# A Mamba-2 mixer and a dequantised FFN in one kernel: the hand-written order of the mixer's steps is replaced

## The chip, the cores and the metric

One core of one Trainium2 chip runs the whole program. The metric is the device time of one execution in microseconds (us), as the median of three runs.

## What is computed

The input is 16 sequences of 256 tokens with 256 features, all in fp32. Each token goes through a Mamba-2 mixer, a residual sum, a layer norm, an FFN, a second residual sum and a second layer norm. The FFN's weights arrive as 4-bit codes with one scale for each block of 32.

```python
z, xBC, dt = split(u @ W_in)
xBC = silu(causal_conv4(xBC) + conv_b)
x, B, C = split(xBC)
dt = softplus(dt + dt_bias)
y = ssd(x * dt, -exp(A_log) * dt, B, C) + x * D
y = y * silu(z)
h = layernorm(u + (rmsnorm(y) * norm_scale) @ W_out)
out = layernorm(h + (gelu(h @ Wg.T) * (h @ Wu.T)) @ Wd.T)
```

Wg, Wu and Wd are the dequantised weights, with 2048 hidden units. The products keep fp32 accuracy: each factor is split into a high part and a rest (`_hi`, `_lo`), and three matmuls replace one (helper `mm3`, lines L540 to L542).

## The kernel before

**Groups.** The tokens are cut into nine groups: FIRST (number -1, one sequence, 2 tiles of 128 tokens), groups 0 to 6 (two sequences, 4 tiles each) and LAST (number 7, 2 tiles). Groups 1 to 6 are the steady ones; 1 to 5 are a hardware loop. While the mixer of group g runs, the FFN of group g-1 runs beside it. A group begins, in this text, where its predecessor's transposes "F1" (L660) stand: they turn the normed rows for the FFN. So the FFN of a 2-tile group runs beside the mixer of group 0.

**Units.** The FFN has 16 units. A unit is, on PE, the products into `gate_bank`, then those into `up_bank`, then the `down` products of the unit two before. ACT makes for it `in_hi` of the unit before (L789) and the GELU of this one (L803); DVE makes `in_lo` of the unit before (L1068) and the product gate times up (L1082). The gate products of unit n wait for the GELU of unit n-1, the up products for DVE's product of unit n-1, the down products for `in_lo`.

**Slots.** The mixer's steps stand by name in `SLOTS`, a list of 17 lists. `stages` turns it into one sequence: slot n, then unit n, slot n+1, unit n+1 and so on. Every engine walks through this one sequence and issues its own part of each step, so a step's place decides the order on all engines at once. Each engine works strictly in its order. The steps are:

- `x4`, `x5`, `x0` to `x3`: one input projection on PE (six matmuls of 512 columns), a bias and first tap on ACT (L738), three convolution taps (L937) and a SiLU (L868, tanh on ACT L722, both a projection or more later) on DVE. The last SiLU hangs on `z3`.
- `z0` to `z3`: one projection on PE, a tanh on ACT (L751), one product on DVE (L950).
- `CB0`, `CB1`: the products of B and C (L579, L581), masked on DVE (L956, L957), one copy on ACT (L757).
- `A`: the running sums (L596, L598), exponentials on ACT (L761, L762), copies on DVE (L962 to L965). SP then writes the sums to DRAM (`spread`, L451) and reads them back broadcast to all partitions as `low` (L460) and `dec` (L465).
- For tile i: `H` eight relus on ACT in place in `dec` (L770), after the landing of `dec`; `L` an addition on DVE (L971); `X` an exponential on ACT (L775); `XT` transposes on PE (L588) and a product on DVE (L976); `W` the product with CB on DVE (L982, L1042, L986); `Y` the products on PE (L607, for odd tiles also L617) and the sums on DVE (L998 to L1005); `g` squares and the split on ACT and DVE (L778, L783, L1009 to L1013); `S` the mean square (L624, L1024, POOL L1175); `op` the output projection and the residual on DVE (L1020).
- `ln1`, `ln2`: the layer norm's statistics and its application (L1050, L1054, POOL L1162 and L1164, L1062).

**Banks.** `USES` gives the order of the 32 products that go through four PSUM banks in turn: use n waits until use n-4 was read. `LINKS` hangs the 22 small steps of softplus (`dt`) between the convolution taps on DVE; the last one, `dA` (L921), releases `A`.

**Weights.** The 24 chunks of FFN weights are dequantised in the first two groups, on items of the same lists: `DECODE` and `VALUE` on DVE (L1106 to L1113, L1124), `UPPER` and `LOWER` on ACT (L810, L814), `TAKE_OFF` on PE (L689, L691). From chunk 13 on, PE's part of chunk c waits for ACT's `LOWER` of chunk c-1. `WOUT_AT` names the step behind which ACT scales and splits the output weights (L829, L832) in FIRST. Four constants set where among SP's scale loads the other transfers of these groups stand.

Of the kernel before, what the change touches and what calls it, by code (L numbers as in the profile page):

```python
# [57 lines left out]
VALUE = {FIRST: {"win": [0, 1], "x5": [2], "x0": [3], "A": [4], "x2": [5], "L0": [6], "XT0": [7], "X1": [8], "g0":
         [9, 10], "g1": [11], "S1": [12]}, 0: {0: [13], "x0": [14], "x1": [15], "CB0": [16], "A": [17,
         18], "L0": [19], "H1": [20], "L1": [21], "L2": [22], "S0": [23]}}  # L60
UPPER = {FIRST: {"win": [0], "x0": [1], "z0": [2, 3], "A": [4], "z3": [5], "W0": [6, 7], "W1": [8], "S0": [9],
         "op0": [10], "op1": [11, 12]}, 0: {"x5": [13], 1: [14], "z1": [15], "x2": [16], 4: [17, 18],
         "X0": [19], 7: [20], "g0": [21], "W2": [22], "g1": [23]}}
TAKE_OFF = {FIRST: {"x4": [0], "x1": [1], "z0": [2], "x3": [3], "z3": [4], "H1": [5], "W1": [6], "Y0": [7], "XT1":
         [8], "g1": [9, 10], "op1": [11], "ln1": [12]}, 0: {"x0": [13], "CB0": [14], "x2": [15], "x3":
         [16], 4: [17], "X0": [18], "Y0": [19], "W1": [20], 9: [21], "XT3": [22], 13: [23]}}
LOWER = {FIRST: {"z0": [0, 1], "x2": [2], "z2": [3], "L0": [4], "X0": [5], "Y1": [6, 7], "S1": [8, 9], "ln1": [10,
         11], "ln2": [12]}, 0: {"z0": [13], "CB1": [14], 3: [15], "x3": [16], "H0": [17], "Y0": [18],
         "H1": [19], "Y1": [20], "Y2": [21], "W3": [22], 14: [23]}}
# [1196 lines left out]
```

How the kernel before makes its waits and increments, by code:

```python
def wait(eng, signal, group, k):  # L125
    value = signal.at(group, k)
    if not isinstance(value, int) or value > 0:
        eng.wait_ge(signal.sem, value)
# [278 lines left out]
        @block.sync  # L408
# [1 line left out]
            def load_block(b):  # L410
                if b:
                    sp.wait_ge(decoded.sem, b)
                sp.dma_start(packed[:, :], ffn_w[:, b, :]).then_inc(packed_in.sem, 16)
# [1 line left out]
            def load_scales(c):  # L415
                if c >= 2:
                    sp.wait_ge(valued.sem, c - 1)
                sp.dma_start(scales[:, c % 2, :], ffn_s[:, c, :]).then_inc(scales_in[c % 2].sem, 16)
# [20 lines left out]
            def wait_for(*rises):  # L439
                values = [s.at(group, k) for s, group, k in rises]
                values = [v if isinstance(v, int) else sp.to_reg(v) for v in values]
                sp.wait_ge(wout_in.sem, 16)
                for (s, _, _), v in zip(rises, values):
                    sp.wait_ge(s.sem, v)
# [1 line left out]
            def spread_sums(g, which=range(NT)):  # L448
# [5 lines left out]
                    if i >= 2:
                        wait_for((exp_in, g, i - 1))
                    elif kind_of(g) == "first" and i:
                        sp.wait_ge(winz_ok.sem, JT)
                    sp.dma_start(low[:, i % 2, :, :], of_tile(1, i).partition_broadcast(P)).then_inc(lo_in[i % 2].sem, 16)
                    if i >= 2:
# [40 lines left out]
                if c == KEEP_FIRST:  # L502
                    sp.wait_ge(wt_lo.sem, BESIDE_FIRST)
                    keep_h(FIRST)
```

## Time and profile before

| | |
|---|---|
| median of three runs | 926.2 us (924.76 to 927.67) |
| the profiled execution's own time | 930.15 us |
| its span, first to last instruction | 928.4 us |
| PE busy | 858.1 us (92%) |
| PE weight loads | 742.8 us (80%) |
| DVE busy | 698.9 us (75%) |
| ACT busy | 554.3 us (60%) |
| POOL busy | 71.4 us (8%) |
| mean granted clock of PE | 0.978 |

Times are counted from the span's first instruction. A duration of PE includes a modelled tail that overlaps the next matmul, so the sum of its durations is more than its busy time, and the distance from one start to the next says how fast it works. "Idle before" is the engine's idle time ahead of a row, and behind it stands what ended it. The clock is the granted one, 1.00 being 2.4 GHz and 0.50 being 1.2 GHz.

### The profile page before, as it was taken

Reading aid. Unit: us, or ns where it says so; the run is one execution under the profiler, and the core shown is the slowest. Engines: PE = TensorE matmul, PEld = TensorE weight load, DVE = VectorE, ACT = ScalarE, POOL = GpSimd, SP = SyncE. Lnnn points to the kernel's source line nnn. Section 1 sums busy time; section 2 is a strip of 40 time slices with the busy share of each in tenths; the row PEclk is TensorE's granted clock in tenths of the full one; section 3 lists DMA queues with packets and bytes.
Section 4 is the critical chain, followed back from the end, with each engine's and each line's share of the span. In section 5 each row is a group of like instructions: output and inputs, shape, how many; then the busy total and the mean of one; then the engine's idle time right before and its main releaser. Section 6 shows DMA issues by size and latency. Waiting matters only on the chain.

```text
span 928.4 us, 16398 instructions
## 1 busy us (share of the span) xinstructions
PE 858.1 (92%) x5512; PEld 742.8 (80%) x5512; DVE 698.9 (75%) x1588; ACT 554.3 (60%) x1014; POOL 71.4 (8%) x105
## 2 busy tenths in 40 slices
PE   4669798899999999999999999999999999999997
PEld 3448677787898888887888789888888788888886
DVE  6776878787879688886878787877879687857453
ACT  4844687458735776548735775559636774566232
POOL 2110000200020000200020000200020000100000
PEclk9897989899999999999999999999999999999999
DMA  4421440015101420023001420133001410130010
GB/s 144 132 76 39 128 124 24 12 58 161 35 24 68 121 85 23 25 75 139 34 23 68 126 79 23 45 90 128 11 23 69 150 57 12 58 104 1 1 35 12
DMA packets 37578, 61.32 MB, mean 66 GB/s; under 512 B 3264, under 2 KB 25888, under 8 KB 37536
## 3 DMA queue, kind: packets, MB, share of 16 engines
q1 hardware_dynamic: 37104, 60.76, 20.5%
q8 instruction: 23, 0.38, 0.2%
q14 instruction: 19, 0.16, 0.1%
q10 hardware_dynamic: 432, 0.03, 0.0%
HBM read 51.94 MB, written 4.64 MB: 61 GB/s over the span
## 4 chain that ended last, share of the span: by engine, by line
PE 65%; DVE 10%; DMA 9%; issue 7%; ACT 5%; POOL 3%; SPq 1%; DVEq 0%; POOLq 0%; ACTq 0%
DMA dec<-spread 7%; PE gate_bank L540 5%; PE up_bank L540 5%; PE up_bank L542 5%; PE up_bank L541 5%; PE gate_bank L542 5%; PE gate_bank L541 5%; PE mixer L540 5%; PE down L540 4%; PE down L541 4%; PE down L542 4%; PE mixer L541 4%; PE mixer L542 4%; PE mixer L607 3%; ACT dec L770 2%
## 5 line engine op out<-in xcount | busy, mean ns | idle before, releaser
L540 PE MATMUL down<-wd_hi,in_hi 128*128 128x256 f32 x512 | 144.1, 282 | 0.7 <-DVE in_lo L1068 0.7
L541 PE MATMUL down<-wd_lo,in_hi 128*128 128x256 f32 x512 | 142.9, 279 | 0.0
L542 PE MATMUL down<-wd_hi,in_lo 128*128 128x256 f32 x512 | 142.6, 278 | 0.0
L937 DVE SCALAR_TENSOR_TENSOR xbc<-mixer,chan,xbc 128x510 f32<-128x510 f32 (+1 forms) x162 | 111.1, 686 | 25.2 <-ACT xbc L738 24.3
L540 PE MATMUL gate_bank<-hT_hi,wg_hi 128*128 128x512 f32 (+1 forms) x288 | 113.2, 393 | 11.4 <-ACT act_sb L803 11.4
L789 ACT ACTIVATE in_hi<-act_sb 128x512 fp32r<-128x512 f32 (+1 forms) x144 | 83.0, 576 | 64.1 <-PE down L542 53.0
L1082 DVE SCALAR_TENSOR_TENSOR act_sb<-up_bank,act_sb 128x512 f32<-128x512 f32 (+1 forms) x144 | 90.6, 629 | 39.9 <-PE up_bank L542 20.0
L1068 DVE TENSOR_TENSOR in_lo<-act_sb,in_hi 128x512 fp32r<-128x512 f32 (+1 forms) x144 | 90.2, 627 | 40.2 <-ACT in_hi L789 39.7
L540 PE MATMUL up_bank<-hT_hi,wu_hi 128*128 128x512 f32 (+1 forms) x288 | 107.0, 371 | 5.6 <-DVE act_sb L1082 5.6
L803 ACT ACTIVATE act_sb<-gate_bank 128x512 f32<-128x512 f32 (+1 forms) x144 | 79.0, 549 | 50.4 <-PE gate_bank L542 49.8
L542 PE MATMUL up_bank<-hT_hi,wu_lo 128*128 128x512 f32 (+1 forms) x288 | 107.0, 371 | 0.0
L542 PE MATMUL gate_bank<-hT_hi,wg_lo 128*128 128x512 f32 (+1 forms) x288 | 106.8, 371 | 0.0
L541 PE MATMUL gate_bank<-hT_lo,wg_hi 128*128 128x512 f32 (+1 forms) x288 | 106.5, 370 | 0.0
L541 PE MATMUL up_bank<-hT_lo,wu_hi 128*128 128x512 f32 (+1 forms) x288 | 106.4, 370 | 0.0
L540 PEld LDWEIGHTS down<-wd_hi,in_hi 128*128 128x128 f32 x512 | 96.9, 189 | 5.1 <-DVE in_lo L1068 1.1
L541 PEld LDWEIGHTS down<-wd_lo,in_hi 128*128 128x128 f32 x512 | 96.9, 189 | 4.3
L542 PEld LDWEIGHTS down<-wd_hi,in_lo 128*128 128x128 f32 x512 | 96.8, 189 | 0.0
L738 ACT ACTIVATE xbc<-mixer,chan 128x512 f32<-128x512 f32 (+1 forms) x54 | 39.5, 731 | 88.8 <-PE mixer L542 88.7
L770 ACT ACTIVATE dec<-dec,sum_hi 128x128 f32<-128x128 f32 x256 | 78.4, 393 | 13.1 <-DMA dec<-spread 13.1
L540 PE MATMUL mixer<-uT_hi,win_hi 128*128 128x512 f32 (+1 forms) x180 | 72.4, 402 | 13.0 <-DVE wdt L1142 9.5
L540 PEld LDWEIGHTS gate_bank<-hT_hi,wg_hi 128*128 128x128 f32 x288 | 54.7, 190 | 25.5 <-ACT act_sb L803 11.4
L1175 POOL TENSOR_TENSOR rms<-rms_v,minus_half 128x1 f32<-128x1 f32 x32 | 18.8, 588 | 710.2 <-DVE rms_v L1024 710.2
(183 smaller groups left out, 1868.5 us busy)
## 6 DMA issues: line engine op xcount, KB each, us to landing
low<-spread SPq DMA_DIRECT2D x32, 512.0 KB, 3.8
dec<-spread SPq DMA_DIRECT2D x32, 512.0 KB, 6.1
state_decay<-spread SPq DMA_DIRECT2D x32, 128.0 KB, 7.4
xbc<-in_u_t_dram SPq DMA_DIRECT2D x7, 512.0 KB, 3.7
h_sb<-in_u_dram SPq DMA_DIRECT2D x7, 512.0 KB, 3.8
h_res<-h_sb SPq DMA_DIRECT2D x7, 512.0 KB, 2.9
out_dram<-h_res SPq DMA_DIRECT2D x7, 512.0 KB, 2.9
scales<-in_ffn_s_dram SPq DMA_DIRECT2D x24, 128.0 KB, 2.2
```

The lines of the kernel that those rows point to most:

```text
L540: nc.tensor.matmul(dst, lh, rh, start=first, stop=False, skip_group_check=True)
L541: nc.tensor.matmul(dst, lh, rl, start=False, stop=False, skip_group_check=True)
L542: return nc.tensor.matmul(dst, ll, rh, start=False, stop=last, skip_group_check=True)
L607: mm = nc.tensor.matmul(bank(g, use)[a * HP:(a + 1) * HP, j * P:(j + 1) * P], xdt[:, h * HP:(h + 1) * HP], dec[:, i % 2, h, :], start=True ...
L738: nc.scalar.activation(xbc[:, i, 0:width(g)], bank(g, f"x{i}")[:, 0:width(g)], ACT.Identity, bias=chan[:, 24 + i:25 + i], scale=chan[:, 18 ...
L770: ins = nc.scalar.activation(at, at, ACT.Relu, bias=sum_hi[:, c:c + 1], scale=-1.0)
L789: nc.scalar.activation(in_hi[:, n % 2, 0:width(f)], act_sb[:, n % 2, 0:width(f)], ACT.Copy)\
L803: nc.scalar.activation(act_sb[:, n % 2, 0:width(f)], GB[:, 0:width(f)], ACT.Gelu_apprx_tanh, scale=CODE_SCALE).then_inc(gelu_ok.sem, 1)
L937: ins = stt(acc[:, :, d:], src[:, :, 0:SEQ - d], chan[:, c:c + 1], acc[:, :, d:], ALU.mult, ALU.add)
L1068: tt(in_lo[at], act_sb[at], f32(in_hi[at]), ALU.subtract)\
L1082: stt(inter, UB[:, 0:width(f)], CODE_SCALE, inter, ALU.mult, ALU.mult)\
L1175: tt(rms[:, i:i + 1], rms_v[:, i:i + 1], half[:, 0:1], ALU.pow).then_inc(rms_ok.sem, 1)
```

## The change

It changes tables only, no instruction's code. In the steady groups (`"full"`) z0 and z1 stand one slot sooner, CB0 one later and CB1 three later, x2 one sooner, z3 one later. H0 stays in slot 5, now behind CB1 and z3, with L0 in the same slot. H1 and H2 stand at the front of their slots, and XT1, L1, g0, L2, X2, H3, op0, g1, S1, op1 and S2 stand one slot sooner. In group 0 (`"second"`) H0 and L0 stand a slot sooner, and S3, op3 and ln1 are in slot 14, with slot 15 empty. FIRST gets a new order too: A and CB0 sooner, z3 ahead of H0, XT0 ahead of L0. The five tables of weight chunks and `LINKS` are written anew for these orders; every chunk is still made once, and chunk block 5 is decoded at the end of FIRST instead of in group 0. LAST is untouched.

```diff
-    "full": ["dt", "x4", "x5", "x0", "z0", "x1", "CB0", "CB1", "z1", "x2", "z2", "A", "x3", "z3", "XT0", "Y0", "XT1",
...
+    "full": ["dt", "x4", "x5", "z0", "x0", "z1", "x1", "x2", "z2", "CB0", "A", "x3", "CB1", "z3", "XT0", "Y0",
...
-    "full": [["x5"], ["x0", "z0"], ["x1", "CB0", "CB1", "z1"], ["x2", "z2"], ["A", "x3", "z3"], ["H0"],
-             ["L0", "XT0", "X0", "W0"], ["Y0", "H1"], ["L1", "XT1", "X1", "W1"], ["Y1", "g0", "H2"],
...
+    "full": [["x5", "z0"], ["x0", "z1"], ["x1", "x2"], ["z2", "CB0"], ["A", "x3"], ["CB1", "z3", "H0", "L0"],
+             ["XT0", "X0", "W0"], ["H1", "Y0", "XT1", "L1"], ["X1", "g0", "W1"], ["H2", "L2", "Y1", "XT2", "X2"],
...
-    "second": [[], ["x5", "x0", "z0"], ["x1", "CB0", "CB1", "z1"], ["x2", "z2"], ["A", "x3"], ["z3"], ["H0",
-               "L0", "XT0", "X0", "W0"], ["Y0", "H1", "L1", "XT1"], ["X1", "W1"], ["Y1", "g0", "H2", "L2",
...
+    "second": [[], ["x5", "z0", "x0"], ["z1", "x1", "x2"], ["z2", "CB0"], ["A", "x3", "CB1", "z3"], ["H0",
+               "L0"], ["XT0", "X0", "W0"], ["H1", "Y0", "XT1", "L1"], ["X1", "g0", "W1", "H2"], ["L2", "Y1",
...
+               ["Y3", "S2"], ["op2", "g3"], ["S3", "op3", "ln1"], [], ["ln2"]],
...
-DECODE = {FIRST: {"win": [1], "x2": [2], "XT1": [3], "S0": [4]}, 0: {"x0": [5], 3: [6], "z3": [7]}}
...
+DECODE = {FIRST: {"win": [1], "A": [2], "L0": [3], "g0": [4], "ln2": [5]}, 0: {"z2": [6], "z3": [7]}}
...
-WOUT_AT = "x3"
...
+WOUT_AT = "X1"
...
-SPREAD_FIRST, NEXT_UT, KEEP_FIRST, SPREAD_NEXT = 6, 14, 15, 20
+SPREAD_FIRST, NEXT_UT, KEEP_FIRST, SPREAD_NEXT = 6, 13, 17, 20
```

The order of ACT's instructions in a steady group, from A's exponentials (L761) on, before:

```order
L761 ACTIVATE xtail<-mixer3 32x128
L762 ACTIVATE low_exp<-mixer3 128x32
L738 ACTIVATE xbc<-mixer0,chan 128x512
L722 ACTIVATE y<-xbc 128x512 x2
L751 ACTIVATE zs<-mixer1 128x512
L789 ACTIVATE in_hi<-act_sb 128x512
L803 ACT_TABLE_LOAD
L803 ACTIVATE act_sb<-gate_bank 128x512
L770 ACTIVATE dec<-dec,sum_hi 128x128 x8
```

and with the change (its lines are one higher, since a line was added to a table):

```order
L762 ACTIVATE xtail<-mixer2 32x128
L763 ACTIVATE low_exp<-mixer2 128x32
L739 ACTIVATE xbc<-mixer3,chan 128x512
L723 ACTIVATE y<-xbc 128x512
L790 ACTIVATE in_hi<-act_sb 128x512
L804 ACT_TABLE_LOAD
L804 ACTIVATE act_sb<-gate_bank 128x512
L758 ACTIVATE cb<-mixer0 128x128
L723 ACTIVATE y<-xbc 128x512
L752 ACTIVATE zs<-mixer1 128x512
L771 ACTIVATE dec<-dec,sum_hi 128x128 x8
```

The GELU of unit 4 stood behind the last tanh and z3's; now these two and CB1's copy stand between it and the relus of tile 0.

DVE's instructions in a steady group between x1's last tap and the product of unit 2 (L1082), before:

```order
L868 SCALAR_TENSOR_TENSOR xbc<-y,xbc 128x512
L956 TENSOR_TENSOR cb<-mixer2,tri 128x128
L957 TENSOR_TENSOR cb<-mixer2,tri 128x128
L956 TENSOR_TENSOR cb<-mixer3,tri 128x128
L957 TENSOR_TENSOR cb<-mixer3,tri 128x128
L950 SCALAR_TENSOR_TENSOR zs<-zs,mixer0 128x512
L908 SCALAR_TENSOR_TENSOR dtp<-dtp,dts 128x32
L1068 TENSOR_TENSOR in_lo<-act_sb,in_hi 128x512
L1082 SCALAR_TENSOR_TENSOR act_sb<-up_bank,act_sb 128x512
```

and with the change:

```order
L869 SCALAR_TENSOR_TENSOR xbc<-y,xbc 128x512
L938 SCALAR_TENSOR_TENSOR xbc<-mixer3,chan,xbc 128x2x255
L907 SCALAR_TENSOR_TENSOR dtp<-dtp,dtq 128x32
L938 SCALAR_TENSOR_TENSOR xbc<-mixer3,chan,xbc 128x2x254
L938 SCALAR_TENSOR_TENSOR xbc<-mixer3,chan,xbc 128x2x253
L909 SCALAR_TENSOR_TENSOR dtp<-dtp,dts 128x32
L869 SCALAR_TENSOR_TENSOR xbc<-y,xbc 128x512
L1069 TENSOR_TENSOR in_lo<-act_sb,in_hi 128x512
L1083 SCALAR_TENSOR_TENSOR act_sb<-up_bank,act_sb 128x512
```

CB0, CB1 and the z product left this place, and the taps and the SiLU of x2 came in.

ACT's instructions in group 0 around the relus of tile 0, before:

```order
L751 ACTIVATE zs<-mixer1 128x512
L789 ACTIVATE in_hi<-act_sb 128x256
L803 ACTIVATE act_sb<-gate_bank 128x256
L770 ACTIVATE dec<-dec,sum_hi 128x128 x8
L814 ACTIVATE wd_lo<-down1 128x512
```

and with the change:

```order
L811 ACTIVATE wd_hi<-act_sb 128x512
L811 ACTIVATE wg_hi<-h_res 128x2x256
L815 ACTIVATE wd_lo<-down1 128x512
L771 ACTIVATE dec<-dec,sum_hi 128x128 x8
L790 ACTIVATE in_hi<-act_sb 128x256
L804 ACTIVATE act_sb<-gate_bank 128x256
```

The copy `wd_lo` of chunk 17, for which PE's part of chunk 18 waits, stood behind the relus and stands ahead of them now; one unit's GELU went the other way.

## Rows read from the trace of the kernel before

**Rows 1.** Busy time by stretch: window, busy and (count) of PE, PEld, DVE, ACT, POOL, clock, DMA.
```profile
0.00:67.70 67.70, 40.00 (x199) 27.60 (x199) 51.05 (x134) 38.64 (x84) 11.04 (x26) 0.92 0.39 117
67.70:172.19 104.49, 88.76 (x575) 74.91 (x575) 79.77 (x189) 67.89 (x135) 9.05 (x10) 0.91 0.24 72
...
379.40:483.00 103.60, 101.10 (x650) 87.84 (x649) 81.74 (x180) 64.82 (x114) 7.85 (x11) 1.00 0.18 66
...
791.70:928.40 136.70, 122.77 (x857) 112.07 (x856) 80.08 (x200) 59.74 (x119) 7.51 (x12) 0.97 0.11 36
```

**Rows 2.** Waits of the whole run: who waited for whom, total us, times, longest.
```profile
PE gate_bank L540 <- ACT act_sb L803: 11.4, 9, 1.7
...
PE mixer L607 <- DVE dec L986: 6.3, 9, 1.1
```

**Rows 3.** Timeline of PE in group 3: start, duration, what, [idle before, released by].
```profile
410.76 0.38 PE L596 MATMUL mixer<-tri,dA 128*96 128x128 f32 x2
...
411.12 0.48 PE L540 MATMUL mixer<-uT_hi,win_hi 128*128 128x512 f32 x1
...
414.01 0.40 PE L540 MATMUL gate_bank<-hT_hi,wg_hi 128*128 128x512 f32 x1
...
419.64 0.50 PE L540 MATMUL gate_bank<-hT_hi,wg_hi 128*128 128x512 f32 x1 [1.33 <-ACT act_sb L803]
...
429.64 1.09 PE L607 MATMUL mixer<-dec,xdt 128*64 128x128 f32 x16 [0.89 <-DVE dec L986]
```

**Rows 4.** Timeline of ACT over the same stretch of group 3.
```profile
411.35 0.27 ACT L761 ACTIVATE xtail<-mixer 32x128 f32<-32x128 f32 x1 [1.25 <-PE mixer L598]
...
416.04 0.63 ACT L722 ACTIVATE y<-xbc 128x512 f32<-128x512 f32 x1 [1.93 <-DVE xbc L937]
...
417.70 1.28 ACT L803 ACT_TABLE_LOAD   x1
418.99 0.60 ACT L803 ACTIVATE act_sb<-gate_bank 128x512 f32<-128x512 f32 x1
420.81 2.46 ACT L770 ACTIVATE dec<-dec,sum_hi 128x128 f32<-128x128 f32 x8 [1.22 <-DMA dec<-spread]
```

**Rows 5.** Timeline of DVE in group 3, 398 to 431 us.
```profile
401.57 0.28 DVE L956 TENSOR_TENSOR cb<-mixer,tri 128x128 f32<-128x128 f32 x1
...
403.66 0.69 DVE L1082 SCALAR_TENSOR_TENSOR act_sb<-up_bank,act_sb 128x512 f32<-128x512 f32 x1
406.23 0.75 DVE L937 SCALAR_TENSOR_TENSOR xbc<-mixer,chan,xbc 128x510 f32<-128x510 f32 x1 [1.88 <-ACT xbc L738]
...
428.27 1.22 DVE L986 TENSOR_TENSOR dec<-dec,cb 128x1024 f32<-128x1024 f32 x1
```

**Rows 6.** Timeline of ACT in group 0, 98 to 124 us.
```profile
113.27 2.45 ACT L770 ACTIVATE dec<-dec,sum_hi 128x128 f32<-128x128 f32 x8 [2.33 <-DMA dec<-spread]
```

**Rows 7.** Timeline of PE in group 0, 98 to 178 us.
```profile
101.32 0.43 PE L596 MATMUL mixer<-tri,dA 128*96 128x128 f32 x2 [1.16 <-DVE dA L921]
...
116.34 2.04 PE L689 MATMUL down<-h_res,ident 128*128 128x512 f32 x2 [3.97 <-ACT wd_lo L814]
...
172.19 1.13 PE L660 MATMUL gate_bank<-ident,h_sb 128*128 128x128 f32 x4 [3.56 <-DVE h_sb L1062]
```

**Rows 8.** Busy time by stretch, after the stall of group 0.
```profile
115.60:122.40 6.80, 6.06 (x21) 4.92 (x21) 5.19 (x8) 6.74 (x13) 0.00 (x0) 0.50 0.19 43
```

**Rows 9.** Timelines at the norm's last step: DVE and POOL in group 0, DVE in group 3.
```profile
168.87 3.27 DVE L1062 TENSOR_SCALAR h_sb<-h_sb,mv,lnr 128x256 f32<-128x256 f32 x4 [0.93 <-POOL lnr L1164]
...
168.99 2.68 POOL L1171 TENSOR_TENSOR uT_lo<-xbc,uT_hi 128x512 fp32r<-128x512 f32 x2 [0.23 <-ACT uT_hi L731]
...
481.33 1.39 DVE L1062 TENSOR_SCALAR h_sb<-h_sb,mv,lnr 128x256 f32<-128x256 f32 x4 [0.36 <-POOL lnr L1164]
```

**Rows 10.** Timelines of ACT, then DVE, in the first group, 30 to 45 us.
```profile
35.06 2.45 ACT L770 ACTIVATE dec<-dec,sum_hi 128x128 f32<-128x128 f32 x8 [0.83 <-DMA dec<-spread]
...
37.84 0.43 DVE L868 SCALAR_TENSOR_TENSOR xbc<-y,xbc 128x256 f32<-128x256 f32 x1 [2.27 <-ACT y L722]
```

More of the change, by code:

```diff
@@ L26 @@
 USES = {
[3 rows of a table removed]
+    "full": ["dt", "x4", "x5", "z0", "x0", "z1", "x1", "x2", "z2", "CB0", "A", "x3", "CB1", "z3", "XT0", "Y0",
+             "XT1", "Y1", "Yoff0", "XT2", "S0", "op0", "Y2", "S1", "XT3", "op1", "Y3", "Yoff1", "S2", "op2",
+             "S3", "op3"],
+    "first": ["dt", "x4", "x5", "x0", "z0", "A", "CB0", "x1", "z1", "x2", "x3", "z2", "z3", "XT0", "Y0", "XT1",
               "Y1", "Yoff0", "S0", "op0", "S1", "op1"],
@@ L56 @@
 BESIDE_FIRST = 13
-DECODE = {FIRST: {"win": [1], "x2": [2], "XT1": [3], "S0": [4]}, 0: {"x0": [5], 3: [6], "z3": [7]}}
[L58 to L69, printed above, removed]
@@ L71 @@
-LINKS = {4: {("x4", 1): [3], ("x4", 2): [4], ("x4", 3): [5], ("x5", 1): [6], ("x5", 2): [7], ("x5", 3): [8],
[2 rows of a table removed]
+DECODE = {FIRST: {"win": [1], "A": [2], "L0": [3], "g0": [4], "ln2": [5]}, 0: {"z2": [6], "z3": [7]}}
+VALUE = {FIRST: {"win": [0, 1], "x5": [2], "x0": [3], "x1": [4], "x3": [5], "X0": [6], "W0": [7], "W1": [8],
+         "XT1": [9], "g0": [10], "g1": [11], "S1": [12]}, 0: {0: [13], "z0": [14, 15], "x1": [16], "A":
+         [17], "CB1": [18], 4: [19], "X0": [20], "H1": [21], "W1": [22], "g1": [23]}}
@@ new lines @@
+UPPER = {FIRST: {"x4": [0], "x0": [1], "A": [2], "CB0": [3], "x3": [4], "L0": [5], "X0": [6], "Y0": [7], "Y1":
+         [8], "g0": [9], "op0": [10], "S1": [11], "op1": [12]}, 0: {"x5": [13], "z1": [14], "z2": [15],
+         "CB1": [16], 4: [17, 18], "X0": [19, 20], 8: [21], "Y2": [22], "S1": [23]}}
+TAKE_OFF = {FIRST: {"x4": [0], "x0": [1], "z1": [2], "x3": [3], "z3": [4], "H1": [5], "W1": [6], "XT1": [7], "Y1":
+         [8], "g1": [9, 10], "ln1": [11, 12]}, 0: {"x0": [13], "x2": [14], "CB0": [15], "z3": [16], 4:
+         [17], 5: [18], "H1": [19], 7: [20], "X2": [21], "Y2": [22], "g2": [23]}}
@@ new lines @@
+LOWER = {FIRST: {"z0": [0], "z1": [1], "z2": [2], "XT0": [3], "H1": [4], "X0": [5], "g0": [6], "op0": [7], "op1":
+         [8, 9, 10], "ln2": [11, 12]}, 0: {"z1": [13], "z2": [14], "CB1": [15], "z3": [16], 4: [17],
+         "XT0": [18], "XT1": [19], "Y1": [20], "op0": [21], "XT3": [22], 11: [23]}}
+LINKS = {4: {("x4", 1): [3], ("x4", 2): [4, 5], ("x5", 1): [6], ("x0", 1): [7], ("x0", 2): [8, 9, 10],
+             ("x0", 3): [11], ("x1", 1): [12], ("x1", 2): [13, 14], ("x2", 1): [15], ("x2", 3): [16], ("z2", 0): [17, 18,
+             19, 20, 21]},
```

15 rows, old and new, of tables (LINKS, SLOTS, USES) are left out of this document.

## The prediction

> **What bounds the kernel now.** I read the busy time by stretch first [rows 1]. The profile's page puts PE at 92% busy, and a steady group shows it plainly: in group 3 PE is busy 101.10 of 103.60 us at a clock of 1.00, DVE 81.74 and ACT 64.82. So in the six steady groups PE sets the time, and all that an order can give back there is PE's idle time, 2.5 us a group. The two groups ahead are another matter: FIRST has PE busy 40.00 of 67.70 us, and DVE with 51.05 is the fullest engine; group 0 has 88.76 of 104.49 at a clock of 0.91. Together they leave over 40 us idle. LAST and the end (136.70 us) are not touched.
>
> The waits name the idle time [rows 2]: PE's gate products wait for a GELU (11.4 us, 9 times) and its Y products for DVE's `dec` (6.3 us, 9 times). PE's timeline shows one of each in group 3 [rows 3]: 1.33 us before the gate products of unit 5, 0.89 us before Y0. Nothing else there is worth a term.
>
> ACT's timeline says why the first comes [rows 4]. After A (411.35) ACT stands before the last tanh (416.04) until DVE has done x3's taps, an idle time of 1.93 us; then z3, `in_hi`, a table load, and only at 418.99 the GELU of unit 4. After it ACT waits 1.22 us more for the landing of `dec` and does tile 0's relus until 423.27.
>
> **The steady groups.** PE's products are the same, so only waits change. I walk through the new order.
>
> *Slot 2.* x1 and x2 now follow each other. DVE loses the two CBs here (four products, each up to 0.28, about 0.8 us) and gains x2's three taps at 0.75 and its SiLU (0.69, the length of the other 512-wide products), about 3.0 us [rows 5]. Its product for unit 2 starts at 403.66 and ends at 404.35; 2.2 us on is 406.6. PE wants it for unit 3's up products. These and the `down` products behind them stand right before A (410.76), and each third of a unit takes 1.4 us: unit 4 begins at 414.01, and 1.33 us of idle time end at 419.64, so it ends at 418.3 [rows 3]. So they begin at about 408.0 now, and at 407.3 without CB1 ahead. Room: 0.7 us. DVE's idle 1.88 us before x2 [rows 5] is what paid for it. Price nothing; the bound is 1.5 us a group, if DVE is late by twice that room.
>
> *Slots 4 and 5.* Unit 4's GELU no longer stands behind the last tanh and z3. The gate products of unit 5 find it done: 1.33 us gone, with the little that PE takes to start again. But the landing of `dec` is now the chain. From A's exponentials (411.35) to the landing (420.81) it is 9.46 us [rows 4], all of it transfers and their waits, and and the new order makes A sooner only by CB1's products on PE. No row prices these alone: between nothing and a projection's 1.45 us (two take 411.12 to 414.01, [rows 3]); with half the columns I take half of it, 0.7. H0 then starts at about 420.1, ends at 422.6, and unit 5's GELU, behind it on ACT as before, ends at 423.6. PE would be there 0.9 us before. So at unit 6's gate products **0.7 us** are won, not 1.33: a new wait of 0.9 us takes the place of the old.
>
> *Y0.* It waited for W0 (428.27, 1.22 us, [rows 5]), which came late behind `in_lo` and the product of unit 5 (0.69 each), both ahead of L0. L0 now stands ahead of them. W0 ends sooner by the 0.7 of the landing and some 0.6 of these two, at 428.2; the rest of Y0's wait is 0.3. PE stands **1.3 us** ahead there.
>
> *Behind it* H2 and H3 wait for transfers that SP may issue only after Y0 and Y1, so they move with them. X2 loses its stand behind Y1 on DVE, and F1 keeps its distance from op3 (same slots). I keep 1.2 of the 1.3: six groups, **-7.2 us**. Bounds: -2.5 each, all of PE's idle time, and +1.5 each from slot 2.
>
> **Group 0.** Two stalls carry it [rows 7]. At 116.34 PE had stood 3.97 us, since chunk 18 waits for ACT's `wd_lo` of chunk 17, which stood behind H0; H0 itself waited 2.33 us for `dec` and took 2.45 [rows 6]. Now that copy is ahead of H0. In its place unit 6's gate products wait for the GELU behind H0. A comes sooner, too: DVE has one chunk block less to decode before it and both CBs, and A had waited 1.16 us for DVE [rows 7]. I take **-3.5** for this: the nearest row is 3.97, less the new wait, plus A's gain. Bounds 0 (the wait only moves) and -7 (with the clock). After the stall the clock stood at 0.50, that is 1.2 GHz, for the whole stretch of 6.80 us, in which PE was busy 6.06 [rows 8]; at 2.4 GHz that work would take 3.0 less. I leave this out of the sum, since a wait of some two us stays in this place.
>
> The Trainium skill, "TensorE: Matmul & The Clock Gate", section "HAM oscillation", says that a wait long enough puts the engine back to half its clock, and that each such wait is paid again in slow matmuls. By that rule a stall that gets shorter wins the slow stretch too: -6.5 for this term where I have -3.5, and 908 for the whole.
>
> The other is at the end: F1 waits 3.56 us for the layer norm [rows 7]. Its last step took 3.27 us for four instructions, against 1.39 in group 3; POOL's `uT_lo` for the next group ran beside it (168.99, 2.68 us) [rows 9]. Now ln1 stands in slot 14 and a unit without mixer work follows, so the norm is done when PE comes and ahead of `uT_lo`. **-3.0**, bounds 0 and -3.6.
>
> **FIRST.** DVE is the chain. It stood 2.27 us before the last SiLU, since ACT did H0's relus (35.06, 2.45) ahead of the tanh [rows 10]. z3 is ahead of H0 now, and ACT's split of the output weights has moved behind X1. Against it, block 5 is decoded here, after ln2, about 1.5 us partly in idle time, and L0 still waits for relus that themselves start later. **-1.5**, bounds -3 and +1.5.
>
> **Sum.** -7.2 - 3.5 - 3.0 - 1.5 = -15.2. The profiled execution took 930.15 us of its own time, so it would take 915.0; it lies 3.95 above the median, and against the median of 926.2 the sum gives **911.0 us**.
>
> **Rivals.**
>
> *The wait only changes its name.* The `dec` transfers land later than 9.46 us after A, since other transfers now meet them, or H3's do. Then the steady groups give nothing and the first two their 8.0: 918.2. For it: three of the five steps on this path are transfers, whose time I can't see inside. Against: their neighbours in the queue don't change. 0.15.
>
> *Slower: DVE becomes the engine that PE waits for in slot 2.* Two sets of taps and two SiLUs run in a row there, with 0.7 us of room. If DVE enters slot 2 more than 0.7 us later than I have it (z0 and z1 are sooner as well), every further tenth is paid by PE at unit 3, and A and with it `dec` slip as well. At 2 us late, 1.3 is paid at unit 3 and the landing takes back the rest: +1.3 for each steady group, +7.8, and in group 0, where DVE is fuller, the 8.0 are lost: 934. It decides from a PE wait before unit 3's up products above 1.2 us. 0.13.
>
> *Nothing in sum:* the steady groups lose what the first two win, 926. 0.07.
>
> *More than I say, by the clock.* The stall in group 0 gets short enough that PE stays at 2.4 GHz, which wins the 3.0 us of [rows 8], and the steady groups win half a us more each, for which the landing of `dec` would have to come 0.5 us sooner: 905. For it: 0.50 stands in the trace right behind the longest wait. Against: another wait remains there. 0.05. The page of the skill named above would have the first half of this happen.
>
> **How the numbers follow.** The forecast itself, from 905 to 917, has 0.60. I call 0.3% (2.8 us) what a measurement of this kernel can tell. Faster is 0.60 + 0.15 + 0.05 = 0.80, less some of the second's weak end: 0.79. Same 0.08, slower 0.13. The range from 903 to 923 takes in the forecast, its bounds up to both clock and a weak DVE, and the first rival; it leaves out the slower one and some of the third.
>
> **What would show it.** In a steady group of the changed kernel: no PE wait before unit 5's gate products, one of about 0.9 before unit 6's, Y0's wait under 0.5, a group 1.2 us shorter than the 103.60 of group 3. In group 0: no PE wait for `wd_lo`, F1's wait under 1 us, its last norm step near 1.4. FIRST ends near 66. I am wrong if a wait for DVE stands before unit 3's up products, if H0's wait for `dec` on ACT grows past 2 us, or if PE waits before F1 in the steady groups.

## The result, and the profile after

The changed kernel takes **910.94 us** (median of 5 runs, 910.7 to 912.51) where the kernel before, timed beside it, takes 927.67 (5 runs, 924.76 to 929.48): ratio 0.9822, 95% interval 0.9804 to 0.9841, so 14.7 to 18.2 us less. A second set gave 912.8 against 927.67 us, ratio 0.9832 (0.9809 to 0.9855). The forecast was 911.0 us, range 903 to 923. The profiled execution took 912.18 us with a span of 910.4, against 930.15 and 928.4.

Busy time by stretch of the changed kernel: FIRST, group 0, group 3, LAST with the end (columns as in [rows 1]; every line number is one higher than before).

```profile
0.00:66.92 66.92, 43.80 (x200) 30.94 (x200) 51.77 (x135) 38.62 (x84) 11.23 (x26) 0.87 0.40 118
66.92:166.75 99.83, 88.62 (x576) 74.54 (x576) 80.45 (x189) 67.52 (x135) 7.30 (x9) 0.91 0.25 76
369.70:471.00 101.30, 100.91 (x649) 87.61 (x649) 82.21 (x180) 65.08 (x114) 8.51 (x11) 1.00 0.21 68
774.70:910.40 135.70, 121.35 (x858) 110.78 (x856) 79.94 (x200) 59.71 (x119) 7.58 (x12) 0.98 0.10 36
```

PE's idle time in group 3 went from 2.50 us (103.60 less 101.10, [rows 1]) to 0.39; the busy times of that group's PE, DVE and ACT are within 0.5 us of what they were. In FIRST PE is busy 3.8 us longer, at a clock of 0.87 where it had 0.92. The 18.0 us between the two spans lie so, by the starts of F1:

| stretch | before | after | difference |
|---|---|---|---|
| FIRST | 67.70 | 66.92 | -0.8 |
| group 0 | 104.49 | 99.83 | -4.7 |
| group 1 | 103.87 | 101.12 | -2.7 |
| groups 2 to 6 | 515.60 | 506.87 | -8.7 |
| LAST and end | 136.74 | 135.70 | -1.0 |

Waits of PE in the whole run (total us, times, longest), the two that [rows 2] shows of before:

```profile
PE gate_bank L541 <- ACT act_sb L804: 4.9, 6, 1.8
PE mixer L608 <- DVE dec L987: 4.7, 4, 2.0
```

The wait for `dec` is gone from the steady groups. Of the six waits for a GELU three still stand there, all before unit 6's gate products: 0.17 us in group 1, 0.59 in group 2 and 0.21 in group 6. PE's timeline of group 3, to be read against [rows 3]: unit 3's up products, then the gate products of units 4, 5 and 6, then Y0.

```profile
397.37 0.50 PE L541 MATMUL up_bank<-hT_hi,wu_hi 128*128 128x512 f32 x1
...
402.09 0.40 PE L541 MATMUL gate_bank<-hT_hi,wg_hi 128*128 128x512 f32 x1
...
408.28 0.40 PE L541 MATMUL gate_bank<-hT_hi,wg_hi 128*128 128x512 f32 x1
...
413.12 0.51 PE L541 MATMUL gate_bank<-hT_hi,wg_hi 128*128 128x512 f32 x1
...
417.72 1.09 PE L608 MATMUL mixer<-dec,xdt 128*64 128x128 f32 x16
```

None has a wait that the view prints; single instructions show 0.09 us at 413.12 and 0.07 at 417.72, where before there were 1.33 ahead of unit 5 and 0.89 ahead of Y0. ACT, against [rows 4]:

```profile
400.83 0.27 ACT L762 ACTIVATE xtail<-mixer 32x128 f32<-32x128 f32 x1 [1.07 <-PE mixer L599]
...
405.42 0.60 ACT L804 ACTIVATE act_sb<-gate_bank 128x512 f32<-128x512 f32 x1
...
409.61 2.46 ACT L771 ACTIVATE dec<-dec,sum_hi 128x128 f32<-128x128 f32 x8 [0.53 <-DMA dec<-spread]
...
412.50 0.57 ACT L804 ACTIVATE act_sb<-gate_bank 128x512 f32<-128x512 f32 x1
```

Unit 4's GELU stands at 405.42, 2.9 us ahead of the gate products that want its bank. From A's exponentials (400.83) to the landing (409.61) it is 8.78 us, 9.46 before. Unit 5's GELU, behind H0, ends at 413.07, and PE is there. DVE, against [rows 5]: the product of unit 2, L0, W0.

```profile
396.63 0.68 DVE L1083 SCALAR_TENSOR_TENSOR act_sb<-up_bank,act_sb 128x512 f32<-128x512 f32 x1
...
412.10 1.23 DVE L972 TENSOR_TENSOR dec<-dec,low 128x1024 f32<-128x1024 f32 x1 [2.30 <-ACT dec L771]
...
416.36 1.22 DVE L987 TENSOR_TENSOR dec<-dec,cb 128x1024 f32<-128x1024 f32 x1
```

The product of unit 2 ends at 397.31 and PE starts unit 3's up products at 397.37. That is the 0.7 us of room of slot 2, used up.

In group 0, PE's waits, against [rows 7]:

```profile
96.39 1.10 PE L690 MATMUL down<-act_sb,ident 128*128 128x512 f32 x2 [1.13 <-ACT wd_lo L815]
...
115.47 0.36 PE L541 MATMUL gate_bank<-hT_hi,wg_hi 128*128 128x256 f32 x1 [1.77 <-ACT act_sb L804]
...
120.47 1.09 PE L608 MATMUL mixer<-dec,xdt 128*64 128x128 f32 x16 [0.90 <-DVE dec L987]
...
130.17 1.09 PE L608 MATMUL mixer<-dec,xdt 128*64 128x128 f32 x16 [2.01 <-DVE dec L987]
...
134.72 2.05 PE L690 MATMUL down<-act_sb,ident 128*128 128x512 f32 x2 [0.94 <-ACT wd_lo L815]
...
166.75 0.74 PE L661 MATMUL gate_bank<-ident,h_sb 128*128 128x128 f32 x4 [0.47 <-DVE h_sb L1063]
```

Chunk 18's wait of 3.97 us is gone, the GELU wait of 1.77 has come in its place, and two waits for `dec` follow. PE also waits four times for ACT's copies of other chunks, 3.4 us in sum: the two rows with `wd_lo`, and 0.60 and 0.76 us at 104.52 and 109.57. F1 waits 0.47 where it waited 3.56. The norm's last step (DVE) and POOL's `uT_lo` there, against [rows 9]:

```profile
165.32 1.37 DVE L1063 TENSOR_SCALAR h_sb<-h_sb,mv,lnr 128x256 f32<-128x256 f32 x4
166.68 2.72 POOL L1172 TENSOR_TENSOR uT_lo<-xbc,uT_hi 128x512 fp32r<-128x512 f32 x2 [2.02 <-ACT uT_hi L732]
```

The step takes 1.37 us and is over before `uT_lo` begins; it took 3.27 beside it.

### The profile page after: what moved, and what is told of

Same layout as the page of the kernel before. It is cut to its first block, busy times and chain, and to the rows that moved or that the text cites. A ratio compares the mean times of both kernels' runs of the same rounds, so it can differ in the third digit from the quotient of the medians.

```text
span 910.4 us, 16399 instructions
## 1 busy us (share of the span) xinstructions
PE 858.1 (94%) x5512; PEld 741.5 (81%) x5512; DVE 703.0 (77%) x1588; ACT 555.9 (61%) x1014; POOL 76.8 (8%) x105
## 4 chain that ended last, share of the span: by engine, by line
PE 71%; DMA 7%; DVE 7%; issue 6%; ACT 5%; POOL 3%; SPq 1%; POOLq 0%; DVEq 0%; ACTq 0%
PE gate_bank L541 6%; PE up_bank L541 5%; PE gate_bank L543 5%; PE up_bank L543 5%; PE gate_bank L542 5%; PE up_bank L542 5%; DMA dec<-spread 5%; PE mixer L541 5%; PE down L541 5%; PE down L542 5%; PE down L543 5%; PE mixer L543 4%; PE mixer L542 4%; PE mixer L608 4%; ACT dec L771 2%
## 5 line engine op out<-in xcount | busy, mean ns | idle before, releaser
L541 PE MATMUL gate_bank<-hT_hi,wg_hi 128*128 128x512 f32 (+1 forms) x288 | 111.0, 386 | 5.1 <-ACT act_sb L804 4.9
L1083 DVE SCALAR_TENSOR_TENSOR act_sb<-up_bank,act_sb 128x512 f32<-128x512 f32 (+1 forms) x144 | 90.3, 627 | 26.7 <-PE up_bank L543 22.1
L541 PE MATMUL mixer<-uT_hi,win_hi 128*128 128x512 f32 (+1 forms) x180 | 72.4, 402 | 12.6 <-DVE wdt L1143 8.8
L1176 POOL TENSOR_TENSOR rms<-rms_v,minus_half 128x1 f32<-128x1 f32 x32 | 23.8, 745 | 675.6 <-DVE rms_v L1025 675.6
L541 PEld LDWEIGHTS up_bank<-hT_hi,wu_hi 128*128 128x128 f32 x288 | 54.4, 189 | 18.5 <-DVE act_sb L1083 9.4
```

The costliest lines, as they stand in the source:

```text
L541: nc.tensor.matmul(dst, lh, rh, start=first, stop=False, skip_group_check=True)
L1083: stt(inter, UB[:, 0:width(f)], CODE_SCALE, inter, ALU.mult, ALU.mult)\
L1176: tt(rms[:, i:i + 1], rms_v[:, i:i + 1], half[:, 0:1], ALU.pow).then_inc(rms_ok.sem, 1)
```

## The experiments

Twelve kernels, all timed in five rounds beside the kernel before. The sets' medians of before are 927.28 us (the first four), 926.56 (the next four) and 927.67 (the last four); ratios are to these.

| kernel | us | ratio to before, 95% interval |
|---|---|---|
| steady groups alone | 918.22 | 0.9904 (0.9889 to 0.9919) |
| first two groups alone | 920.24 | 0.9925 (0.9911 to 0.9938) |
| norm of group 0 late | 917.44 | 0.9895 (0.988 to 0.991) |
| L0 late | 916.86 | 0.9887 (0.9872 to 0.9902) |
| z3 beside A | 913.84 | 0.9861 (0.984 to 0.9882) |
| `wd_lo` of chunk 17 behind H0 | 913.23 | 0.9857 (0.9836 to 0.9878) |
| CB0 in slot 2 | 913.88 | 0.9866 (0.9848 to 0.9885) |
| LAST with A early | 907.27 | 0.9789 (0.977 to 0.9808) |
| the change again | 912.8 | 0.9832 (0.9809 to 0.9855) |
| H0 early in FIRST | 915.58 | 0.9864 (0.9844 to 0.9884) |
| block 5 decoded later | 914.76 | 0.9859 (0.984 to 0.9879) |
| LAST with slot 0 empty | 904.6 | 0.975 (0.9733 to 0.9767) |

### The two halves apart

The first kernel is the one before with the change's "full" lists (slots, banks, links) for groups 1 to 6; group 0 keeps its own. The second is the change with the old "full" lists for groups 1 to 6.

```diff
+def uses_of(g):
+    return "second" if isinstance(g, int) and g == 0 else kind_of(g)
...
-            return MB[USES[kind_of(g)].index(use) % 4]
+            return MB[USES[uses_of(g)].index(use) % 4]
```

> The new order in the six steady groups alone; FIRST, group 0, LAST as before. Theory (the parts are local and add up): groups 1 to 6 lose their idle time as in the changed kernel, 103.3 to 101.3 us in groups 2 to 6 and 1.0 in group 1, whose slow stretch behind F1's wait of 3.56 us stays: -9.7, so 917.5 against 927.2 us, ratio 0.9895. Rival 1 (only my forecast's 1.2 a group is the order's, the rest of what the changed kernel won came from a luckier landing of the dec transfers): 920, ratio 0.992. Rival 2 (the steady groups' gain hangs on the slow stretch being gone): groups 2 to 6 above 102.5 us each.

> The new lists for FIRST and group 0 (mixer steps and chunks) alone; groups 1 to 6 in their old order. Theory (the slow clock goes with the wait before F1): FIRST 66.9, group 0 99.8 and group 1 shorter by 1.7 through the clock, -7.2: 920.0 us, ratio 0.992. Rival (waits alone, the slow stretch comes anyway): -5.5, 921.7 and a granted clock of 0.5 somewhere from 165 to 175 us. Groups 2 to 6 stand at 103.3 with their 1.33 us before unit 5's gate products in both.

They gave -9.1 and -7.0 us, against -9.7 and -7.2 expected. The product of the ratios is 0.9830, the whole change 0.9822 and 0.9832: the halves add. Groups 1 and 3 of the steady groups alone:

```profile
171.20:276.90 105.70, 105.43 (x642) 91.91 (x643) 80.49 (x172) 64.72 (x113) 5.45 (x8) 0.94 0.19 64
...
378.90:480.30 101.40, 100.89 (x649) 87.63 (x648) 82.17 (x180) 65.06 (x114) 8.51 (x10) 1.00 0.21 68
```

Group 3 is as short as in the change, and groups 2 to 6 take 101.3 to 102.0 us, so neither rival of the first kernel holds. Group 1 is at 0.94: the wait of 3.56 us before F1 is there, and this time the clock stood at 0.50 from 169.9 to 183.6. With the first two alone that wait is 0.47 and no slow stretch stands anywhere near it, against the rival: group 1 took 102.92 us, 103.87 before, though PE's waits in it (2.02 us before, F1's left out) came to 2.89. So the clock gave back 1.8 (103.87 - 2.02 less 102.92 - 2.89).

### The norm of group 0

```diff
-["Y3", "S2"], ["op2", "g3"], ["S3", "op3", "ln1"], [], ["ln2"]]
+["Y3", "S2"], ["op2", "g3"], [], ["S3", "op3", "ln1"], ["ln2"]]
```

> The changed kernel with S3, op3 and ln1 of group 0 back in slot 15 and slot 14 left empty. Theory (the norm's place made F1's wait and the slow clock behind it): PE waits 3.0 to 3.6 us before F1, POOL's uT_lo stands beside the norm's last step, which takes about 3.3 us, and a stretch at 0.5 follows: +3.1 and +1.7, 915.7 us. Rival 1 (the stretch does not follow): +3.1, 914.0. Rival 2 (the wait was gone for another reason, DVE being ahead in the new order): under 1 us of wait, 911 to 912.

PE at F1, DVE's norm step, POOL's `uT_lo`, and the stretch at half clock, which begins in F1's wait and ends 4.6 us behind it:

```profile
169.29 1.12 PE L661 MATMUL gate_bank<-ident,h_sb 128*128 128x128 f32 x4 [3.56 <-DVE h_sb L1063]
```

```profile
165.96 3.27 DVE L1063 TENSOR_SCALAR h_sb<-h_sb,mv,lnr 128x256 f32<-128x256 f32 x4 [0.93 <-POOL lnr L1165]
```

```profile
166.09 2.68 POOL L1172 TENSOR_TENSOR uT_lo<-xbc,uT_hi 128x512 fp32r<-128x512 f32 x2 [0.23 <-ACT uT_hi L732]
```

```profile
167.10:173.90 6.80, 4.61 (x19) 4.32 (x20) 5.09 (x10) 1.20 (x2) 1.66 (x2) 0.50 0.00 0
```

All four came back with one edit: the wait of 3.56, the step of 3.27 and the overlap to the hundredth, and the half clock. Rivals 1 and 2 are out. In the fourteen traces of this study a slow stretch stands around F1 at the end of group 0 in the three where F1 waited 3.56 us (before, steady groups alone, this one) and in none of the eleven where it waited 0.5. The time rose by 6 us (ratio 0.9895 against 0.9822 and 0.9832) where 4.8 was expected; of the rest, 1.1 us of this trace lie in LAST, see below.

### The steady groups: what holds each wait away

```diff
-["CB1", "z3", "H0", "L0"], ["XT0", "X0", "W0"]
+["CB1", "z3", "H0"], ["L0", "XT0", "X0", "W0"]
```

> The changed kernel with L0 of tile 0 of the steady groups behind in_lo and the product of unit 5, as it was before. Theory (ACT's table load covers part of it: the exp could not start before 414.38 anyway, and L0 would end at about 415.05): W0 is 0.7 us later, PE waits 0.8 before Y0 in each of the six groups: +4.3, 915.2 us. Rival 1 (the two DVE instructions count in full with the gap before them, 1.7 us): +9.5, 920.4. Rival 2 (L0's place is worth nothing, PE takes the time elsewhere): 911 to 911.5.

```diff
-["A", "x3"], ["CB1", "z3", "H0", "L0"]
+["A", "x3", "CB1", "z3"], ["H0", "L0"]
```

> The changed kernel with CB1 and z3 of the steady groups back in slot 4, ahead of unit 4's products; H0 and L0 stay. Theory (the last tanh and z3 ahead of unit 4's GELU on ACT made the wait before unit 5's gate products, and dec lands as before, so PE has no slack at Y0): a PE wait of about 0.8 us before unit 5's gate products (1.33 less CB1's 0.57 of PE work that now stands ahead of it), the 0.1 waits before unit 6's and Y0 gone, +0.65 in each of six groups: +4, 915 us. Rival 1 (the place of z3 is worth its whole old wait): 1.33 each, +8, 919. Rival 2 (only where H0 and L0 stand counts; the wait before unit 5 is then taken out of those behind it): 911 to 912.

```diff
-["x1", "x2"], ["z2", "CB0"]
+["x1", "x2", "CB0"], ["z2"]
```

> The changed kernel with CB0 of the steady groups back in slot 2, behind x2: DVE gets two products of 0.28 us more there. In the trace of the changed kernel DVE ends the product of unit 2 at 397.31 and PE begins unit 3's up products at 397.37, so the room is nearly gone where my forecast had 0.7. Theory (no room): PE waits about 0.35 us before unit 3's up products in each of six groups, +2.1, 913.0 us. Rival (room of 0.7 as forecast, CB0 costs nothing): 911. A rival past both (A slips too and dec lands later, it is paid twice): 915.

With L0 late, PE's wait before Y0 is 0.87 to 0.89 us in each of the six groups (0.8 expected), and the sum of that name over the run is

```profile
PE mixer L608 <- DVE dec L987: 9.8, 10, 2.0
```

where the change has 4.7. Rivals 1 (1.7 us each) and 2 (nothing) are out; the time is 5 to 6 us above the change by the ratios, 4.3 expected. With z3 beside A, and with CB0 in slot 2, one line each from group 3:

```profile
408.20 0.50 PE L541 MATMUL gate_bank<-hT_hi,wg_hi 128*128 128x512 f32 x1 [0.64 <-ACT act_sb L804]
```

```profile
395.90 0.50 PE L558 MATMUL up_bank<-hT_hi,wu_hi 128*128 128x512 f32 x1 [0.31 <-DVE act_sb L1100]
```

0.64 us before unit 5's gate products (0.8 expected), the waits before Y0 gone; 0.31 before unit 3's up products (0.35 expected), where neither kernel had one. The second stands in groups 2 to 5 (0.29 to 0.31); in groups 1 and 6 the view prints none. The times are 913.84 and 913.88, +3 to +4 by the ratios, where +4 and +2 were expected; their intervals overlap with that of the change in the second set, so it is the two lines that decide. PE's waits in groups 1 to 6 rose by 2.2 and 1.8 us. Each of the three edits puts a price on the path at once. The new order stands where three chains reach PE at nearly the same time as it gets there: DVE's products in slot 2, the GELU behind the last tanh, and `dec`.

### Group 0: the copy and H0

```diff
-"z3": [16], 4: [17],
+"z3": [16], "H0": [17],
```

> The changed kernel with ACT's wd_lo copy of chunk 17 back behind H0 of group 0. My forecast (this edit is what took the wait of 3.97 us away): PE waits 2 to 4 us more for wd_lo at chunk 18 and the clock falls behind it: 914 to 918 us. Theory now (unit 5's GELU stands behind H0 on ACT as well and PE waits for it next, 1.77 us at 115.47, so the copy only adds its own length of 0.6 and the transposes that are pushed behind it): +1 to +1.5, 912 to 912.5. Rival (nothing at all, all of it taken out of the GELU wait): 911.

PE, then ACT, of this kernel:

```profile
114.41 2.04 PE L690 MATMUL down<-h_res,ident 128*128 128x512 f32 x2 [2.66 <-ACT wd_lo L815]
...
122.17 1.09 PE L608 MATMUL mixer<-dec,xdt 128*64 128x128 f32 x16 [1.22 <-DVE dec L987]
```

```profile
111.34 2.44 ACT L771 ACTIVATE dec<-dec,sum_hi 128x128 f32<-128x128 f32 x8 [1.73 <-DMA dec<-spread]
113.69 0.57 ACT L815 ACTIVATE wd_lo<-down 128x512 fp32r<-128x512 f32 x1
```

The wait for chunk 18 is back with 2.66 us, and another stands before Y0, 1.22. The group takes 101.70 us, and its part ahead of F1's wait 101.19, where the ten kernels with the change's lists for the first two groups take 98.11 in the mean (96.93 to 99.74, F1's wait left out): +3.1. The time rose by 2 to 3 us; 913.23 lies between the two expectations, 914 to 918 and 912 to 912.5. My forecast's mechanism stands, and the "theory now" of +1 to +1.5, by which the GELU wait would have taken most of it, is too low.

### FIRST, and block 5

```diff
-"z2", "z3", "H0", "XT0",        WOUT_AT = "X1"
+"z2", "H0", "z3", "XT0",        WOUT_AT = "x3"
```

> The changed kernel with H0 ahead of z3 in FIRST and ACT's split of the output weights back at x3, as both stood before. My forecast (DVE's 2.27 us of idle time before the last SiLU come back): FIRST 1.5 us longer, +1.5, 912.4 us. Rival (DVE is full in FIRST, 51 of 67 us in both kernels, and its other waits give back what this one costs): FIRST within 0.5 us from the point where DVE has a_neg, 911.

```diff
-DECODE = {FIRST: {..., "g0": [4], "ln2": [5]}, 0: {"z2": [6], ...
+DECODE = {FIRST: {..., "g0": [4]}, 0: {"x5": [5], "z2": [6], ...
```

> The changed kernel with the decoding of block 5 moved from behind ln2 of FIRST to behind x5 of group 0. Theory (behind ln2 it costs nothing, because PE then waits 1.9 us for POOL's uT_lo anyway; behind x5 its 1.5 us stand ahead of DVE's work for unit 0): +0.5 to +1.5, 911.5 to 912.5 us. Rival (as my forecast had it, it costs FIRST a part of its 1.5 us, and group 0 has room): -0.5 to -1, 910.

> The changed kernel itself once more, as the yardstick of the others in this set. 910.9 us as measured, within 1.5.

FIRST begins with loads whose arrival differs from run to run (DVE's first use of `a_neg` stands at 12.90 to 13.91 us), so I count from there to F1: 53.80 and 53.78 us in the two traces with the old list, 53.40 in the mean of the ten with the new one, which go from 52.58 to 54.22. With H0 and the split as before it is 56.63. PE's waits in it include the first two rows, and DVE's wait before the last SiLU is back (2.27 before, [rows 10]; none in the change):

```profile
35.17 0.50 PE L692 MATMUL gate_bank<-wu_hi,in_hi 128*128 128x512 f32 x1 [2.80 <-ACT wu_hi L811]
39.11 1.09 PE L589 MATMUL mixer<-ident,xbc 128*128 128x128 f32 x4 [3.44 <-DVE xbc L869]
...
38.54 0.42 DVE L869 SCALAR_TENSOR_TENSOR xbc<-y,xbc 128x256 f32<-128x256 f32 x1 [2.69 <-ACT y L723]
```

against 1.61 before the second in the change. So the places of H0 and of ACT's split together are worth 3.2 us of FIRST (the time: 915.58 against 912.8 in the same set); yet the whole list won 0.4, less than the spread of the ten. Something else in it costs some 2.8 us. Block 5 is not what cost it: with its decoding moved to group 0 FIRST is no shorter (54.38), group 0 is at 100.94 with a new wait of 1.47 us before an up product for DVE, and the time is 914.76, 2 us more (0.5 to 1.5 expected). Behind ln2 it is free. A part may be the clock: it stood at 0.50 for 10.2 and 13.7 us of FIRST with the old list, and for 13.7 to 20.5 with the new one. The two new ones at 13.7 take 52.6 and 52.7 us, the seven at 17.1 take 53.1 to 54.2, and the one at 20.5 takes 54.0. What makes the stretches longer, and which moves cost the rest, wasn't tried.

### LAST in the new order

LAST keeps its old list in the change. Two lists for it, on top of the change:

```diff
 "last":
-[["x5"], ["x0", "z0"], ["x1", "CB0", "z1"], ["x2", "z2"], ["A", "x3", "z3"], ["H0"], ["L0", "XT0", ...
+[["x5", "z0"], ["x0", "z1"], ["x1", "x2"], ["A", "z2", "CB0"], ["x3"], ["z3", "H0", "L0"], ["XT0", ...
```

> The changed kernel with LAST in the new order too, and A there a slot sooner than in the steady groups (LAST has half the mixer work of PE, so the transfers take more units than there). Theory (the same chain of A, transfers, relus, L0, W0 makes the waits of LAST: 0.55 and 1.63 us before gate products, 0.89 before Y0): they fall to under 0.6 in sum, -2.4, 908.5 us; the 2.23 us before unit 1's up products stay. Rival 1 (GELU and table loads on ACT make them, not the transfers): only Y0's goes, 910. Rival 2 (DVE is late in slot 2 with two sets of taps and PE waits 1 us or more before unit 3's up products): 911 to 912.

```diff
-[["x5", "z0"], ["x0", "z1"], ["x1", "x2"], ["A", "z2", "CB0"], ["x3"], ["z3", "H0", "L0"],
+[[], ["x5", "z0"], ["x0", "z1", "x1"], ["A", "x2", "z2"], ["CB0", "x3"], ["z3", "H0", "L0"],
```

> The changed kernel with LAST in the new order, its slot 0 empty, x5 to x1 pushed one slot on, and A in slot 3. Against the list with A early and x5 in slot 0 (907.3 us), which keeps a PE wait of 1.87 us before unit 1's up products, since DVE does x5's taps, z0 and the final norm ahead of unit 0's product. Theory (that queue on DVE makes the wait): the wait goes, 905.4 us. Rival 1 (the same work makes PE wait a unit later, before unit 2's up products): 907. Rival 2 (the final norm alone makes it): a wait over 1 us stays before unit 1's, 907.

Busy time of LAST in the first of these, then PE's only wait there, and LAST in the second:

```profile
773.40:860.90 87.50, 85.63 (x554) 76.29 (x553) 58.77 (x142) 46.54 (x85) 5.42 (x8) 0.98 0.13 43
```

```profile
786.36 0.52 PE L541 MATMUL up_bank<-hT_hi,wu_hi 128*128 128x512 f32 x1 [1.87 <-DVE act_sb L1083]
```

```profile
773.20:857.60 84.40, 84.40 (x555) 75.11 (x554) 58.41 (x142) 46.23 (x85) 5.44 (x8) 1.00 0.14 45
```

With A early the waits of 0.55 and 1.63 us before gate products and 0.89 before Y0 are all gone, as the transfers' chain says (the whole list changed, and A's place in it wasn't tried by itself), and the time is 907.27 us (908.5 expected); with slot 0 empty the last one goes too, and PE is busy 84.40 of 84.40 us. LAST takes 90.42 us in the change, 87.53 and 84.36 here. **904.6 us** (905.4 expected) is the fastest kernel of the study, 2.5% under the one before.

These traces also say what the -1.0 us of LAST in the table above is. A stretch of 3.4 us at half clock begins 12.6 to 13.9 us into LAST in eight of the thirteen traces that have a wait (1.87 to 2.23 us) before unit 1's up products. Seven of them have the old list of LAST, the kernel before among them, and LAST takes 91.4 to 92.4 us; five more with the same list, the change among them, have no such stretch, and LAST takes 90.3 to 90.4. Four of the seven have the change's lists but for one of the small edits above. The change's own two traces lack the stretch and the three with an old half have it, so whether that is chance or the order isn't shown; I don't count the 1.0 as won. In the one trace without the wait there is none.

## Why the prediction was right

The time is right (911.0 against 910.94 us), and so is the size of the sum: 15.2 us forecast, 14.7 to 18.2 measured, 18.0 between the two profiled executions. That the two times agree to 0.1 us is luck. The forecast took its sum from 926.2 us, where the kernel before came to 927.67 beside the change, and errors of 1 to 2 us in its terms cancel. Of the signs it gave, two did not come: the wait of 0.9 us before unit 6's gate products, and no PE wait for `wd_lo` in group 0, where two others remain. The terms, one by one:

**Steady groups: right in mechanism, too small in size.** Forecast -7.2. PE's waits in groups 1 to 6 (F1's left out) fell from 13.0 to 3.6 us, -9.4 (3.4 to 5.3 us remain in the nine traces with these lists untouched), and the new lists alone gave -9.1. The step that was mis-sized is the landing of `dec`: I started from group 3's 9.46 us. Over groups 1 to 6 that interval is 8.80 to 9.46 us before (mean 9.11) and 8.73 to 9.28 after (mean 8.90); group 3 was the latest of the six. The 8.90 is itself low: the other eleven traces with the new steady order, or nearly it, have means of 9.0 to 9.2. Counted from F1, H0 started at 39.9 us where I had 40.7. PE's own arrival at unit 6 was right to 0.05 us (43.35 from F1, 43.3 forecast), so the 0.9 us wait that I put there was 0.09, and Y0's 0.07. Group 2, where the landing took 9.28, shows the forecast's wait at 0.59.

**Slot 2: nothing, as priced, and by a hair.** I gave it 0.7 us of room, it has 0.06: counted from F1, DVE ended the product of unit 2 at 27.63 us where I had 27.2, and PE was there at 27.69 where I had 27.9. Which step of DVE made the 0.4 I haven't traced. CB0 there costs 0.31 at once, so the slower rival's mechanism was nearer than my 0.7 said.

**Group 0, middle: -3.5 forecast, -1.6 in this trace, -2.5 from the mean of the two traces with the old lists to that of the ten.** The step that failed is "the nearest row is 3.97, less the new wait, plus A's gain". The GELU wait came with 1.3 to 1.9 us as foreseen. In no step of mine were tile 1's `dec` (2.01 before 130.17; 2.9 us of waits before Y products, 1.1 before) and the four waits for ACT's copies of other chunks, 3.4 us. Nor did A's gain arrive in this trace: A's exponentials came 0.7 us sooner in the group, and H0's relus 0.2. So the waits, F1's left out, fell only from 12.2 to 10.7 us here, and from a mean of 11.9 to 11.2. The rest of the 2.5 is PE's busy time and goes with the clock, which stood at 0.50 for 17.1 us of the group in both traces with the old lists and for 10.2 to 17.1 in the ten, 13.0 in the mean. Group 0 with the first two groups' lists alone shows it, against 88.76 us busy at 0.91 in [rows 1]:

```profile
66.63:164.94 98.31, 85.96 (x576) 72.75 (x576) 80.44 (x189) 67.55 (x135) 7.29 (x9) 0.95 0.25 77
```

Its waits are 11.9 us, hardly less than before; what it won lies in the clock. Why some traces have less of the slow stretches than others with the same lists isn't settled. Undoing the copy's place alone costs 3.

**Group 0, end: -3.0 forecast, -3.09 for the wait, and -1.8 more that I left out.** The norm step is 1.37 us, as forecast 1.4. What I had kept out of the sum for the middle belonged here: the clock at 0.50 around F1, from 170.2 to 177.0, in which PE was busy 4.81 of 6.80 us before:

```profile
170.20:177.00 6.80, 4.81 (x20) 4.51 (x21) 5.09 (x11) 1.20 (x2) 1.47 (x2) 0.50 0.00 0
```

It went with the wait and came back with it. The rule of the Trainium skill, "TensorE: Matmul & The Clock Gate", section "HAM oscillation", is what the traces agree with here: a long wait is paid a second time in slow matmuls. In the middle of group 0, where I had weighed it, the longest wait is still 1.9 to 2.7 us, and ten of the twelve traces with the new list have a slow stretch somewhere from 99 to 140 us.

**FIRST: wrong in size.** -1.5 forecast, -0.4 measured, which the spread of the ten does not tell from nothing; the 0.8 of the table is mostly the arrival of its loads (`a_neg` at 13.29, 13.91 before). The step "block 5 is decoded here, about 1.5 us partly in idle time" cost nothing, the places of H0 and of ACT's split are worth twice the -1.5, and something else in the list, or the longer time at half clock, takes it back.

Against the sum by terms, then: -9.4 - 2.5 - 3.1 - 1.8 - 0.4 = -17.2, within the interval of 14.7 to 18.2. Two errors of 2 us, the steady groups and the clock, were on the low side, and two of 1 on the high side. None of the rivals happened as told. The one by the clock (905) had a part of it right: its 3.0 us were to come from the middle of group 0, and the clock gave 1.8 behind F1 and some 1.8 spread over group 0, the latter inside the -2.5.

## What to carry to other kernels

A reordering is worth what is left after the next chain arrives: read for each wait how long the next engine in line still has, and read the chain that sets it (here the landing of a transfer) over all repetitions and not in one group, since 0.7 us of spread was most of the wait that I forecast. Before a wait is priced, look at the clock behind it: the wait of 3.56 us cost 1.8 more. After the change, split what a stretch won into waits and busy time: in the middle of group 0 most of the waits had only moved. When an order has been found for the loop, try it in the last pass as well; it has less mixer work and the same chain of transfers. The new order with A a slot sooner and an empty slot 0 won another 6 to 8 us here.

## What was not expected of the hardware

- Four DVE instructions of the norm (128x256, one input from SBUF) take 3.27 us beside POOL's two-input `uT_lo`, in all three traces in which they meet, and 1.37 to 1.39 in every other group of four tiles in all fourteen. It is the second and the third of the four that take 1.35 us each in place of 0.41. POOL's two instructions take 2.68 us there and 2.72 alone, so here DVE alone pays. The Trainium skill, "GPSIMD Engine Reference", section "8. Key points", says that the two engines share their ways into SBUF, and that GpSimd contends with DVE instructions that run in a mode with two ports or read two inputs from SBUF. The traces agree that they contend; whether these ran in such a mode no trace shows.
- The granted clock falls behind shorter waits too: 3.4 us at 0.50 behind a wait of 1.87 or 2.23 us in LAST in eight of thirteen traces, and not in the other five, of the same work. What decides between them isn't settled.
- The landing of `dec`, the same transfers in the same order, came from 8.71 to 9.72 us after A's exponentials in the steady groups of all the traces, and differs between the turns of one loop. Its cause is open.
